# Cross-attention kernel: the low parts of 64 channels made in place by GpSimd and carried to their partitions by small transfers

## The reference

```
# x: (8, 64, 256) latents, ctx: (8, 1601, 192), mask: (8, 1601)
xn = layernorm(ctx, ln_x_g, ln_x_b);  ln = layernorm(_layernorm(x), ln_l_g, ln_l_b)
q = ln @ Wq.T
kv = concatenate([xn @ Wkv.T, ln @ Wlkv.T], axis=1);  k, v = kv[..., :256], kv[..., 256:]
# 4 heads of 64
qn = rmsnorm(q, qn_g) * 64 ** -0.5;   kn = rmsnorm(k, kn_g)    # x / max(rms(x), 1e-8) * gamma
attn = softmax(where(mask, einsum('bhid,bhjd->bhij', qn, kn), -max))
x = x + einsum('bhij,bhjd->bhid', attn, v).reshape(8, 64, 256) @ Wo.T + bo
x = x + rwkv6(_layernorm(x));  x = x + moe(_layernorm(x))
```

## Time and profile before

| | |
|---|---|
| median of 3 runs | 520.67 us |
| the profiled execution | 520.81 us |
| its span | 519.0 us |
| TensorE busy | 431.1 us (83%) |
| VectorE busy | 405.3 us (78%) |
| GpSimd busy | 250.3 us (48%) |
| ScalarE busy | 237.8 us (46%) |
| L1388, the 112 subtractions | 48.0 us, mean 428 ns |
| ACT idle before L1108, for the DMA of the deviations | 33.6 us, 7 times |

### The profile page before, as it was taken

One profiled execution on the slowest core, in us unless ns is written; L12 is line 12 of the kernel. 1 busy time (PEld: TensorE's weight loads), 2 busy tenths in 40 slices (PEclk: granted clock), 3 DMA queues, 4 the chain that ended last, 5 costly groups with the idle time before them and its releaser, 6 DMA issues.

```text
span 519.0 us, 6624 instructions
## 1 busy us (share of the span) xinstructions
PE 431.1 (83%) x2042; PEld 334.5 (64%) x2042; DVE 405.3 (78%) x969; ACT 237.8 (46%) x547; POOL 250.3 (48%) x264
## 2 busy tenths in 40 slices
PE   3786557779799889887998988887997877899996
PEld 0364335567677677675786867774474765678885
DVE  5847799999999999999988896625659556887776
ACT  0238645267466564664654744331233125335551
POOL 5451956658558557576484553001431232445550
PEclk9999988889999999999899999899999988889999
DMA  8605842022141041222200000920000000000001
GB/s 248 179 1 148 237 135 56 2 90 53 51 141 50 3 141 50 76 67 58 90 3 1 1 1 15 406 97 0 0 2 0 1 0 0 1 1 1 0 2 41
DMA packets 23976, 31.80 MB, mean 61 GB/s; under 512 B 2955, under 2 KB 19653, under 8 KB 23941
## 3 DMA queue, kind: packets, MB, share of 16 engines
q1 hardware_dynamic: 23940, 31.38, 19.6%
HBM read 30.69 MB, written 0.52 MB: 60 GB/s over the span
## 4 chain that ended last, share of the span: by engine, by line
DVE 34%; PE 30%; POOL 21%; issue 8%; ACT 4%; DMA 2%; SPq 1%; DVEq 0%; POOLq 0%; ACTq 0%
PE bank L573 29%; POOL kr L483 12%; DVE kss L1397 5%; DVE arena L1409 4%; DVE arena L1445 3%; DVE split_b L1388 3%; POOL crs L448 3%; DVE cst L1334 2%; DVE arena L1604 2%; DVE arena L1618 1%; DVE kguard L1400 1%; POOL split_b L472 1%; DVE big L1319 1%; POOL cguard L449 1%; DMA mask_in<-in_p_mask 1%
## 5 line engine op out<-in xcount | busy, mean ns | idle before, releaser
L573 PE MATMUL bank<-keyq,split_b 128*128 128x512 f32 (+2 forms) x724 | 171.0, 384 | 21.2 <-DVE split_b L1678 6.7
L573 PEld LDWEIGHTS bank<-keyq,split_b 128*128 128x128 f32 (+1 forms) x724 | 124.7, 194 | 51.3 <-issue 18.0
L483 POOL TENSOR_TENSOR kr<-kguard,neg_half 128x8 f32<-128x8 f32 (+1 forms) x56 | 94.4, 1686 | 103.5 <-DVE kguard L1400 103.1
L573 PE MATMUL bank<-arena 128*128 128x193 f32 (+4 forms) x528 | 103.4, 340 | 18.5 <-ACT arena L1133 9.0
L573 PEld LDWEIGHTS bank<-arena 128*128 128x128 f32 (+2 forms) x528 | 86.9, 195 | 31.1 <-issue 13.9
L1126 ACT ACTIVATE arena<-bank 128x512 f32<-128x512 f32 (+1 forms) x56 | 31.5, 563 | 59.9 <-PE bank L573 59.4
L573 PE MATMUL bank<-split_b,keyq 128*128 128x512 f32 x204 | 51.7, 405 | 0.1
L1409 DVE TENSOR_TENSOR arena<-bank,kr 128x512 f32<-128x512 f32 (+1 forms) x56 | 36.1, 645 | 19.3 <-POOL kr L483 19.1
L1388 DVE TENSOR_TENSOR split_b<-arena,split_b 32x256 fp32r<-32x256 f32 (+1 forms) x112 | 48.0, 428 | 2.5
L573 PEld LDWEIGHTS bank<-split_b,keyq 128*128 128x128 f32 x204 | 39.1, 197 | 8.0 <-DVE split_b L1669 0.2
L472 POOL TENSOR_TENSOR split_b<-arena,split_b 128x256 fp32r<-128x256 f32 (+1 forms) x56 | 38.2, 682 | 10.1 <-ACT split_b L1109 10.0
(11 more groups left out here) (222 smaller groups left out, 620.5 us busy)
## 6 DMA issues: line engine op xcount, KB each, us to landing
arena<-in_ctx SPq DMA_DIRECT2D x16, 576.0 KB, 4.4
arena<-in_p_ctxT SPq DMA_DIRECT2D x8, 800.5 KB, 6.7
arena<-in_p_ctxT SPq DMA_DIRECT2D x8, 400.2 KB, 7.1
arena<-in_p_experts SPq DMA_DIRECT2D x1, 2688.0 KB, 18.4
arena<-in_p_experts SPq DMA_DIRECT2D x1, 2304.0 KB, 12.2
arena<-in_p_experts SPq DMA_DIRECT2D x1, 1536.0 KB, 6.4
X<-in_x SPq DMA_DIRECT2D x1, 512.0 KB, 3.7
arena<-in_t_Wlkv SPq DMA_DIRECT2D x1, 512.0 KB, 7.0
```

What stands on the lines that cost most here:

```text
L483: pool.tensor_tensor(kr[0:r, n % 2, 0:k], kg_[0:r, n % 2, 0:k], neg_half[0:r, 0:4 * k].rearrange("p (t h) -> p t h", h=H), ALU.pow).then_i ...
L573: return nc.tensor.matmul(out_, l, r, start=start, stop=stop, skip_group_check=shared)
```

## The change

DVE loses `split_side`. POOL makes the low part of the 64 channels in one subtraction on their own partitions 0 to 63, into a new tile `side_low` (two buffers), right behind `split_rest`. ACT then issues two transfers (`move_side`) that carry 32 partitions each to partitions 96 to 127; `keys(n)` waits for both landings. `split_high` is cut in two: the 128 channels, and the 64 channels (`split_small`). At g = 5 `split_small` stands behind `square_keys`, and only it waits for the deviations. Besides, the factor 1/64 of the mean square and the guard are folded: `cguard` and its multiplication on POOL go, the guard is made of `cve` in the instruction that was there, and the factor 64 ** -0.5 leaves `qkg` and comes back where the latent scores are evacuated.

```
-        cguard = sb("cguard", [P, 2, FULL + 1])
+        side_low = sb("side_low", [SMALL, 2, 256], F32R)
...
 # POOL, context_scales
                 then(pool.tensor_tensor(crs[:, k, of], cve[:, k, of], neg_half[:, 0:n], ALU.pow))
-                then(pool.tensor_scalar(cguard[:, k, of], cve[:, k, of], 1e-16, None, ALU.mult))
...
 # POOL, split_rest(n)
                 pool.tensor_tensor(v[:, 1, 0:k], raw[:, 0], v[:, 0, 0:k].bitcast(F32), ALU.subtract).then_inc(xs_rest, 1)
+                pool.wait_ge(xs_small, n + 1)
+                if n >= 2:
+                    pool.wait_ge(side_in[(n - 2) % 3], 32 * ((n - 2) // 3 + 1))
+                pool.tensor_tensor(side_low[:, n % 2, 0:k], raw[0:SMALL, 1], v[0:SMALL, 2, 0:k].bitcast(F32), ALU.subtract).then_inc(xs_side, 1)
...
 # PE, keys(n)
                 pe.wait_ge(xs_rest, n + 1)
-                pe.wait_ge(xs_side, n + 1)
+                pe.wait_ge(side_in[n % 3], 32 * (n // 3 + 1))
...
 # ACT, split_high(n)
-                    act.wait_ge(sd_in[b % 2], 32 * (b // 2 + 1))
...
-                A(xs[n % 3][:, 0, 0:k], ctxT[b % 2][:, 0, 256 * g:256 * g + k], ACT.Copy)
-                A(xs[n % 3][0:96, 2:4, 0:k], ctxT[b % 2][0:96, 1:2, 256 * g:256 * g + k].broadcast_to([96, 2, k]), ACT.Copy).then_inc(xs_split, 1)
+                A(xs[n % 3][:, 0, 0:k], ctxT[b % 2][:, 0, 256 * g:256 * g + k], ACT.Copy).then_inc(xs_split, 1)
+
+            def split_small(n):
+
+                b, g = divmod(n, NG)
+                if g == 0:
+                    act.wait_ge(sd_in[b % 2], 32 * (b // 2 + 1))
+                k = 256 if g < NG - 1 else TAIL
+                A(xs[n % 3][0:96, 2:4, 0:k], ctxT[b % 2][0:96, 1:2, 256 * g:256 * g + k].broadcast_to([96, 2, k]), ACT.Copy).then_inc(xs_small, 1)
+
+            def move_side(n):
+
+                k = 256 if n % NG < NG - 1 else TAIL
+                act.wait_ge(xs_side, n + 1)
+                for j in range(2):
+                    act.dma_start(xs[n % 3][96:P, 2 + j, 0:k].bitcast(F32), side_low[32 * j:32 * j + 32, n % 2, 0:k].bitcast(F32)).then_inc(side_in[n % 3], 16)
...
 # ACT, before the loop and in it
-            split_high(0)
-            split_high(1)
+            for n in range(2):
+                split_high(n)
+                split_small(n)
+            for n in range(2):
+                move_side(n)
...
                 if u + 2 < groups:
                     split_high(u + 2)
+                    if g != 5:
+                        split_small(u + 2)
...
                 if u < groups:
                     square_keys(u)
+                if g == 5 and u + 2 < groups:
+                    split_small(u + 2)
+                if u + 2 < groups:
+                    move_side(u + 2)
...
 # DVE, key_sums(n); split_side(n) and its three calls go
-                V.scalar_tensor_tensor(kg_[0:r, n % 2, 0:k], kss[0:r, n % 2, 0:k], 1.0 / DH,
-                                       cguard[0:r, b % 2, 2 * g:2 * g + k].unsqueeze(2).broadcast_to([r, k, H]), ALU.mult, ALU.max).then_inc(k_ss, 1)
+                V.scalar_tensor_tensor(kg_[0:r, n % 2, 0:k], cve[0:r, b % 2, 2 * g:2 * g + k].unsqueeze(2).broadcast_to([r, k, H]), DH * 1e-16,
+                                       kss[0:r, n % 2, 0:k], ALU.mult, ALU.max).then_inc(k_ss, 1)
```

More of the change, by code:

```diff
@@ L237, in build @@
         sdT_mm = sem("sdT_mm"); sdT_evac = sem("sdT_evac")
-        sd_rest = sem("sd_rest"); xs_split = sem("xs_split"); xs_rest = sem("xs_rest"); xs_side = sem("xs_side")
+        sd_rest = sem("sd_rest"); xs_split = sem("xs_split"); xs_rest = sem("xs_rest"); xs_small = sem("xs_small"); xs_side = sem("xs_side"); side_in = [sem(f"side_in{i}") for i in range(3)]
         k_mm = sem("k_mm"); k_sq = sem("k_sq"); k_ss = sem("k_ss"); k_r = sem("k_r"); s_norm = sem("s_norm"); s_max = sem("s_max")
@@ L1148, in evac_latent_scores @@
                     act.wait_ge(y_mm, b - 3)
[L1149 removed]
+                A(lat_tile(b), spare_bank(b)[lat_rows(b), 0:D], ACT.Copy, scale=DH ** -0.5).then_inc(ls_evac, 1)
             def evac_turned_sum(b):
@@ L1379, in refold_low_part @@
                 last.then_inc(refold_low, 1)
-            def split_side(n):
-                b, g = divmod(n, NG)
-                dve.wait_ge(xs_split, n + 1)
-                k = 256 if g < NG - 1 else TAIL
-                v, side_ = xs[n % 3], ctxT[b % 2][:, 1, 256 * g:256 * g + k]
-                for j in range(2):
-                    last = V.tensor_tensor(v[96:P, 2 + j, 0:k], side_[32 * j:32 * j + 32], v[32 * j:32 * j + 32, 2 + j, 0:k].bitcast(F32), ALU.subtract)
-                last.then_inc(xs_side, 1)
             def key_sums(n):
@@ L1549, in _ @@
                     shift_scores(u - SHIFT)
-                if u + 2 < groups:
-                    split_side(u + 2)
                 if u + LEAD < groups:
```

5 lines of the change are left out of this document (1 added, 4 removed).

## The result

The changed kernel takes 545.8 us (median; 538.8 to 546.8) against 522.0 us of the kernel before on the same chip: ratio 1.043, interval 1.033 to 1.052. The forecast was 518, with 505 to 535 as range. The execution that was profiled took 546.8 us, with a span of 545.0.

A forecast was written before the change was run, and what follows sets the result against it. VectorE looked like the bound, but step by step either its subtraction or GpSimd's power (kr) ended last. 2.3 won less 2.0 collision, taken as 0.4 us a batch, 8 x 0.4 - 0.3 = 2.9 less: 518 us, range 505 to 535.

The forecast's parts named there:

- g1: Steps g0 to g6 are named by the group whose product of the scores closes them; for g1 0 was forecast.
- What the removal gives: Cross-attention loop: taking the subtractions from DVE, judged step by step, saves 2.3 us a batch.
- The collision: POOL's new subtraction holds DVE's maximum behind g2, g4, g5 and g6: 4 x 0.51 = 2.0 us a batch.
- The rival of no collision: DVE's maximum wins the race or POOL's reads fall between DVE's: 503 us, 510 with half the collisions; chance 31%.
- The rival of a collision everywhere: Maximum held in six steps for the full 0.73, costing 4.4 against 2.3 us a batch: 538 us; chance 23%.
- Eight times the middle batch: Whole loop: the gain of 0.4 us a batch taken 8 times, less 0.3 at the start, gives 2.9.
- hidden, with 0.6 to spare: ACT's hold at move_side around g1: sums and guard end at 198.4, before POOL can start g2's power at 199.05.
- ACT or the transfer becomes late: Rival: at 0.83 an issue ACT is late in g1 and g3, some 1 us a batch: 527 us; chance 7%.
- Two of the signs: Prediction wrong if PE waits for the transfer, squares come late for the sums, or an ACT issue exceeds 0.8 us.
- The transfer: Operand for the keys: lands 2.0 us after issue, with cover of 3.4 us; late only if landing rose to 5.4.
- The later wait for the deviations: At g5 the split that waits for the deviations stands behind the square: worth 0.
- The start: Before the loop: folds about 2.5 us later, DVE loses 2.18 us of subtractions; net +0.3.

The follow-up runs named there:

- e13: Changed kernel with VectorE making the low parts and the deviations waited for where they were before, so only the fold is left: 518.0 us, ratio 0.992.
- e1: Changed kernel with the low parts back on VectorE, without GpSimd's subtraction and the transfers; fold and later wait stay: 520.7 us, ratio 0.996.
- e15: Same program as e1, run again with more rounds: 518.5 us, ratio 0.9955.
- e9: Changed kernel without any low part of the 64 channels: nobody subtracts, nothing is transferred: 497.1 us, ratio 0.952.
- e10: As e9, plus GpSimd's subtraction behind split_rest, its result neither moved nor used: 523.5 us, ratio 1.002.
- e12: Changed kernel with transfers issued one step later and TensorE not waiting for their landing: 524.7 us, ratio 1.004.
- e4: Changed kernel, TensorE doesn't wait for the landing; subtraction, ACT's wait and transfers stay: 536.6 us, ratio 1.025.
- e14: As e4, but the transfers read a tile of zeros and don't wait for GpSimd's subtraction: 522.6 us, ratio 0.998.
- e3: Kernel before with two added free transfers a step on ACT, to spare memory, without waiting for GpSimd: 523.0 us, ratio 1.001.
- e6: Kernel before with GpSimd's unused subtraction behind split_rest, and eight unused TensorE products where it waits for csd: 545.5 us, against 543.3 without the products.
- e5: Changed kernel with the two transfers of a group issued one step later on ACT: 538.2 us, ratio 1.028.

## Why the prediction was wrong, step by step

The ladder of runs, from the kernel before (522.0 to 523.7):

| kernel | us | what the rung adds |
|---|---|---|
| e13, fold alone | 518.0 | -4 to -5: a guard less on GpSimd |
| e1 and e15, later wait too | 518.5 to 520.7 | 0 to +3 |
| e9, no low part | 497.1 | -21 to -24: VectorE's subtractions |
| e10, GpSimd subtracts | 523.5 | +26.3: the collision, and GpSimd's time in g1 and g2 |
| e12, transfers a step late, landing not waited for | 524.7 | +1.2 |
| e4, transfers in their place, landing not waited for | 536.6 | +11.9: ACT's wait |
| after, landing waited for | 545.8 | +9.2: late landings |

The last two rungs hold a part that isn't tied to their cause. Against e14, the same kernel without the wait, the profiled execution of e4 is 2.3 us longer ahead of the first product of the scores, 8.0 in the loop and 3.1 behind it; from e4 to the changed kernel these are 1.4, 6.6 and 2.7. The parts behind the loop are no larger than what e1 and e15 show for one and the same program (3.3).

And the steps, as means over batches 2 to 5 (of "after", batches 3 and 5, and 2 and 4):

| step | before | e9 | e10 | after, 3 and 5 | after, 2 and 4 |
|---|---|---|---|---|---|
| g0 | 5.08 | 4.95 | 5.43 | 5.64 | 5.99 |
| g1 | 5.38 | 4.67 | 5.31 | 5.33 | 5.26 |
| g2 | 5.24 | 4.69 | 5.51 | 5.62 | 5.64 |
| g3 | 5.45 | 4.41 | 4.89 | 4.87 | 4.88 |
| g4 | 4.53 | 4.53 | 4.53 | 4.73 | 5.85 |
| g5 | 4.80 | 4.57 | 5.06 | 4.57 | 4.61 |
| g6 | 4.71 | 3.66 | 4.15 | 4.36 | 4.49 |
| batch | 35.18 | 31.48 | 34.88 | 35.12 | 36.71 |

**What the removal gives: right in place, a little small.** Forecast were 0.9 in g3, 0.8 in g6, 0.2 each in g5 and g0, and 0 in g4. From e13 to e9 they measure 1.00, 1.05, 0.23, 0.13 and 0.00. Missed was g1, where 0.45 was to be had; g2 grew by 0.10. (The 0 and 0.2 forecast for these two can't be set beside that, since they count the guard against the new subtraction; see the next paragraph.)

**The collision: right in kind and price; the balance came out partly by luck.** It was priced at 0.51 in the steps behind g2, g4, g5 and g6; from e9 to e10 these grow by 0.48, 0.49, 0.49 and 0.48. g1 and g2, netted against the guard that went away, were forecast at 0 and -0.2 and came out at -0.07 and +0.27. The sum forecast for DVE and GpSimd was 0.4 us less a batch; e10 has 0.30 less. Two errors cancel in it: against the kernel before, g3 and g6 are 0.56 shorter each where 0.4 and 0.3 net were forecast, and g2 is 0.47 worse than forecast. The changed kernel itself shows only in part the sign that was named (1.2 in g2, g4 and g5, 0.69 elsewhere): its maxima take 1.17 to 1.18 us behind g2, but also 1.21 to 1.27 behind g1 in three batches of four, 0.87 to 1.04 behind g5, and 0.69 behind g4. The rule that the Trainium skill gives in "SBUF — State Buffer", section "Who interferes with whom", which the prediction cited, is borne out three ways: a subtraction holds the maximum (1.17), a fill that reads nothing does not (0.69), and the product that reads PSUM is not held (0.69). The hold is a little shorter than "until the first is done": the subtraction at 201.50 ends at 202.22, so the maximum that starts at 201.61 would take 1.30 us, and it takes 1.17. The rival of no collision falls. The rival of a collision everywhere came nearest to the time (538), but its mechanism, 0.73 in each step from the shift behind the maximum, is not what is there: the held maxima cost 0.5 each.

**Eight times the middle batch: the first step that failed.** The balance holds in batches 2 to 5 only. In e10 batches 6 and 7 take 37.34 and 34.54 instead of 35.41 and 31.98, 4.5 us more together. Those 4.5 us are more than the whole difference of the two profiled spans (3.4). The prediction never looked at a step of the last two batches. In batch 6 GpSimd has one more power to make (`rs`, 0.73 us), and in step g2 it makes that, the rest, the new subtraction and the scales in one row. The guard of DVE is ready at 268.88; the power that waits for it starts 2.5 us later, and DVE stands for it. In e10:

```profile
271.42 1.64 POOL L486 TENSOR_TENSOR kr<-kguard,neg_half 128x8 f32<-128x8 f32 x1
...
273.09 0.69 DVE L1414 TENSOR_TENSOR arena<-bank,kr 128x512 f32<-128x512 f32 x1 [3.60 <-POOL kr L486]
```

That step takes 6.93 instead of 5.83, and g4 behind it 5.56 instead of 4.56, with a square that is 0.8 late. Of batch 7's growth 1.5 us are its step g5 (6.37 against 4.89), where the keys took 3.66 us at a lower clock. It isn't the subtraction's: e14 has 4.92 there with the same subtraction, and e13 has 6.48 without it.

**ACT: the step that failed most.** The prediction took the pair of issues as 0.92 of ACT's time, and asked whether ACT had that time. It had: ACT is 44% busy, and e3 and e14 show that issues cost nothing. The pair measures 1.16 us, 0.58 each, between the two bounds. What cost 12 to 14 us (of them 3.1 behind the loop, see above) is what the prediction set at "hidden, with 0.6 to spare": the wait. It was worked out for one step, g1, and there it is hidden indeed (5.33 and 5.26 against 5.31 in e10). Queued behind a holding `move_side` the prediction named the next high parts and the exponentials, and left out the evacuations of the deviations (g4), the turned sum and the heads, for which TensorE waits at once. Those are the new rows of the waits. It also took the wait and the issues as separate sums, when a wait takes away the cover that the issues had. The rival *ACT or the transfer becomes late* had this path, at 7% and 527: it looked for it in issues of 0.83 us, which cost nothing. Two of the signs that the prediction named for its own failure came true: TensorE waited for the transfer (8.2 us), and squares came late for the sums (18.5 us).

**The transfer: right in the middle batches, wrong beside bulk loads.** The landing was taken as 2.0 us, from one row, with late as the case above 5.4. The median is 1.9; the worst, 6.6, is above 5.4, and costs 8.2 us of TensorE at one place. The prediction looked at the traffic of the transfer (small), not at the traffic that it would meet.

**The later wait for the deviations: right at 0**, or slightly against. In the changed kernel it also moves the new subtraction behind g4: that one waits for the late split of the 64 channels and starts at 188.72, the maximum before it at 187.92 takes 0.69, and g5 is 4.57 instead of e10's 5.06. The fold's "as many instructions" was right for DVE and ACT; its worth on GpSimd was counted in g1 and g2 only as a trade against the new subtraction. Alone it is 0.9 us a batch.

**The start: +0.3 forecast, +2.5 found.** The first product of the scores stands at 57.06 in the changed kernel, at 55.63 in e4 (no landing waited for) and at 53.58 in e12 (one pair fewer ahead of the folds too): the landing and ACT's wait, again.

**The share of the clock** was in no step. The changed kernel's granted clock is 0.922 against 0.964. In the middle batches the runs separate it. A lower clock alone costs nothing: e14 and e6 show that for g4, whose keys had cover. By this count ACT's wait alone costs 0.7 us a batch: batches 3 and 5 of the changed kernel, where the keys of g4 kept the full clock, take 35.12, 0.24 more than e10, and 0.49 more is hidden by the collision that is spared in g5. Both together cost most: in batches 2 and 4, with the lower clock at those keys, g4 takes 5.85 instead of 4.73, and the batch 36.71. The remaining 0.5 us of these batches lies mostly in g0 (5.99 against 5.64) and isn't explained. Why the clock fell in one batch and not in the next, with 1.07 and 0.79 us of idling just before, no run here shows, nor how much of the 12 and 9 us in the start and in batches 0, 1, 6 and 7 would be left at full clock. Behind the loop 6.1 us stand beside a lower clock with the same program, and 3.3 of such a difference appear between e1 and e15, which are one program.

## What to carry to other kernels

When work moves to another engine, price the wait and not only the instructions: list everything that is queued behind the waiting instruction in every step, evacuations first, and ask who waits for each. Two engines that are released by the same event run side by side from there; look at what each reads in that order before a second operation is put on one of them. A small transfer whose landing somebody waits for must be set against the largest bulk load that can be under way, not against its own size.

## What the runs showed of the hardware

- A GpSimd fill of 0.71 us beside a maximum of VectorE over two SBUF tiles leaves it at 0.69 us; a subtraction of 0.72 us that starts 0.1 us ahead makes it 1.17 us, so that it ends 0.56 us after the subtraction (e10, 201.50 and 201.61). VectorE's product of PSUM and SBUF stays at 0.69 us beside such a subtraction.
- ScalarE's queue issues a transfer of 32 partitions by 1 KB in 0.51 to 0.61 us as a rule (median 0.60 in the changed kernel), and this can lie beside its own arithmetic: in e14 the issue at 198.15 beside the square at 198.23. Where the issue stood behind a semaphore wait in the changed kernel (214.44), the arithmetic ahead was over, and both issues were idle time of the engine (1.62 us with the wait).
- The ten key products of two tiles take 2.57 us at full clock (batch 3) and 3.75 us where the granted clock is 0.50 for most of them (batch 4).
- A transfer of 32 KB inside the chip that lands in 1.9 us took up to 6.6 us (changed kernel) and 8.8 us (e5) beside bulk loads on another queue.
